# A two-layer transformer kernel on eight cores: short query tiles placed between long ones, one background piece per place, and the FFN's statistics a chunk earlier

## The reference, cut to what matters

```python
x = x + _layernorm(_L0_attn_ref(_layernorm(x), W))       # one head of width 1024
x = x + _layernorm(_L0_ffn_ref(_layernorm(x), ...))      # 1024 -> 4096 -> 1024, ternary weights
x = x + _layernorm(_L1_attn_ref(_layernorm(x), ...))     # 8 heads, causal, low-rank keys and values
x = x + _layernorm(_L1_ffn_ref(_layernorm(x), ...))      # as the layer-0 FFN, without biases

# layer 0 attention
q, k, v = jnp.split(jnp.einsum('bsd,df->bsf', x, W), 3, axis=-1)
scores = jnp.triu(jnp.einsum('bqd,bkd->bqk', q, k), k=0)
scores = jnp.where(scores == 0, MASK_NEG, scores)
out = jnp.einsum('bqk,bkd->bqd', jax.nn.softmax(scores, axis=-1), v)

# both FFNs: activations rounded to 8 bits by row, weights rounded to -1, 0, 1
scale = 127.0 / jnp.clip(jnp.max(jnp.abs(x), axis=-1, keepdims=True), EPS, None)
wq = jnp.clip(jnp.round(w / jnp.clip(jnp.mean(jnp.abs(w)), EPS, None)), -1.0, 1.0)
```

## Time and profile before

| what | value |
|---|---|
| median of 3 runs | 4179.68 us (4170.07 to 4267.94) |
| the profiled execution | 4174.65 us, its slowest core spans 4172.9 us |
| the eight cores' spans | 4144.4 to 4172.9 us |
| PE busy | 3486.8 us, 84% of the span |
| DVE busy | 2526.8 us, 61% |
| ACT busy | 1602.2 us, 38% |
| POOL busy | 900.0 us, 22% |

### The profile page before, as it was taken

How to read it: one execution, slowest core, us unless ns; L and a number is a source line. 1 busy time by engine, 2 the same in 40 slices (tenths; PEclk the granted TensorE clock), 3 DMA queues, 4 the chain that set the end, 5 groups by cost and what they waited for, 6 DMA issues and landing times.

```text
span 4172.9 us, 52221 instructions; the slowest of 8 cores (4144.4 to 4172.9 us)
## 1 busy us (share of the span) xinstructions
PE 3486.8 (84%) x16088; PEld 1544.3 (37%) x16088; DVE 2526.8 (61%) x3358; ACT 1602.2 (38%) x2230; POOL 900.0 (22%) x1111
## 2 busy tenths in 40 slices
PE   4979799872987889989826788878999699999998
PEld 1433344331333333434313333333443244444443
DVE  2423333333775667767656687877883566666674
ACT  3235554541233443334303455656778111111111
POOL 1101011123232223322224332212112111111111
PEclk9989899986998999999958899999999899999999
DMA  8558686775667788557433212122100344333332
GB/s 239 124 120 194 178 198 191 212 188 173 158 158 143 143 160 167 146 142 164 119 97 92 73 61 77 55 71 73 35 23 32 74 89 88 89 82 83 91 81 59
DMA packets 641614, 494.85 MB, mean 119 GB/s; under 512 B 536512, under 2 KB 561088, under 8 KB 640960
## 3 DMA queue, kind: packets, MB, share of 16 engines
q1 hardware_dynamic: 574752, 331.03, 34.4%
q10 hardware_dynamic: 66592, 160.49, 14.0%
HBM read 277.91 MB, written 84.93 MB: 87 GB/s over the span
## 4 chain that ended last, share of the span: by engine, by line
PE 56%; DMA 11%; DVE 10%; DVEq 6%; issue 5%; ACT 5%; POOL 3%; SPq 2%; ACTq 1%; POOLq 0%
PE psS L1358 15%; PE psO L1423 11%; PE psP L1423 10%; DVEq L1085 6%; PE psS L797 4%; PE psP L901 4%; DVE a_mx L806 3%; PE psS L410 3%; DMA a_onT<-a_on 2%; DMA hqT<-hq 2%; PE psO L881 2%; PE psO L481 2%; DMA b_stg<-w1T 2%; ACT b_stg L1118 1%; PE psP L881 1%
## 5 line engine op out<-in xcount | busy, mean ns | idle before, releaser
L806 DVE TENSOR_REDUCE a_mx<-psS 128x1 f32<-128x1024 f32 (+3 forms) x536 | 632.8, 1203 | 184.3 <-PE psS L797 142.2
L1358 PE MATMUL psS<-big,xqT 128*128 128x512 fp8e4 x2048 | 466.1, 387 | 129.9 <-DVE h L1368 76.1
L889 ACT ACTIVATE a_pT<-psO 128x512 bf16<-128x512 f32 x704 | 400.0, 598 | 225.7 <-PE psO L881 204.6
L1358 PE MATMUL psS<-a_w1q,xqT 128*128 128x512 fp8e4 x2048 | 449.0, 380 | 31.1 <-DMA xqT<-xq 28.4
L1376 ACT ACTIVATE h<-psS,st 128x1024 f32<-128x1024 f32 x128 | 142.5, 1114 | 713.9 <-PE psS L1358 641.7
L1384 DVE TENSOR_REDUCE st<-h 128x1 f32<-128x1024 f32 x256 | 304.8, 1210 | 142.5 <-ACT h L1376 142.5
L797 PE MATMUL psS<-a_kTm,a_qz 128*128 128x512 bf16 (+3 forms) x1152 | 336.1, 376 | 63.5 <-DVE a_mx L806 48.5
L410 PE MATMUL psS<-big,b_zT 128*128 128x512 bf16 (+3 forms) x1152 | 274.5, 397 | 110.9 <-ACT b_zb L391 68.6
L1358 PEld LDWEIGHTS psS<-big,xqT 128*128 128x128 bf16 x2048 | 200.1, 99 | 389.7 <-issue 167.5
L901 PE MATMUL psP<-a_pT,a_vz 128*128 128x512 bf16 x1056 | 327.0, 389 | 0.1
L1373 ACT ACTIVATE h<-h 128x1024 f32<-128x1024 f32 x128 | 135.2, 1057 | 490.3 <-DVE h L1368 487.3
(11 more groups left out here) (194 smaller groups left out, 5045.8 us busy)
## 6 DMA issues: line engine op xcount, KB each, us to landing
b_stg<-w1T ACTq DMA_DIRECT2D x64, 512.0 KB, 5.0
b_stg<-w2T ACTq DMA_DIRECT2D x64, 512.0 KB, 5.0
xt<-xres SPq DMA_DIRECT2D x64, 512.0 KB, 4.8
stg<-w1T ACTq DMA_DIRECT2D x64, 512.0 KB, 5.1
stg<-w2T ACTq DMA_DIRECT2D x64, 512.0 KB, 4.5
b_xt<-x SPq DMA_DIRECT2D x32, 512.0 KB, 5.5
b_xr<-x SPq DMA_DIRECT2D x32, 512.0 KB, 5.6
xres<-b_yz SPq DMA_DIRECT2D x32, 512.0 KB, 3.6
```

The source lines that it names most:

```text
L806: pair_free[k] = [put("v", lambda e: e.tensor_reduce(out=dst, in_=view(ps), axis=AX.X, op=ALU.max), [mm, mx_free.get(i - 2)], "v")]
L889: st_free[n] = put("s", lambda e, g=g, n=n: e.activation(out=pT[p][:, g * 512:g * 512 + 512], in_=stp[n], func=AF.Exp, bias=0.0, scale=1.0 ...
L1358: mm = put("t", lambda e, half_=half_, dc=dc: e.matmul(ps[:, half_ * 512:half_ * 512 + 512], xqT[k][:, dc, :], w1q[:, dc, c * 1024 + half_ ...
```

## The change

- The 32 tiles are visited in the order 0 to 7, then 8, 31, 9, 30, ... 15, 24, then 16 to 23 (`order`; everything is indexed by the place n, and `i = order[n]` is the tile). Where the next tile has more chunks left than the present one offers places for, its chunks are issued together ahead of the present tile's last product (`nxt`).
- `background()` runs at 144 places: after each `form_z`, after each `scores` that isn't a tile's last, after each `weigh` and after each `finish_tile`; at each it advances by 130/144 of a piece.
- `ternary` uses as many staging buffers as it gets: four in layer 0 attention, and still two in the FFN. To make room `xr` and `yz` have one buffer each.
- The four `load_w1` are issued at places 25 to 28 and wait for place 23's last scores.
- In the FFN, of both layers, `front` is split: `front_stats(t+2)` (two bn_stats, aggregate, POOL's operations) is issued at chunk 0 behind `epilogue(t-2)`; the normalising stays at chunk 1.

```diff
-                xr = [sb("xr%d" % k, [128, D], F32, ph) for k in range(2)]
-                yz = [sb("yz%d" % k, [128, D], F32, ph) for k in range(2)]
+                xr = sb("xr", [128, D], F32, ph)
+                yz = sb("yz", [128, D], F32, ph)
-                stg = [sb("stg%d" % k, [128, 1024], F32, ph) for k in range(2)]
+                stg = [sb("stg%d" % k, [128, 1024], F32, ph) for k in range(4)]
+                if NT == 32:
+                    order = list(range(8))
+                    for k in range(8):
+                        order += [8 + k, 31 - k]
+                    order += range(16, 24)
+                else:
+                    order = list(range(NT))
+                total = sum(NC - 1 - (128 * i) // CW for i in range(NT)) + 3 * NT
-                def background(cols):
-                    paid[0] += 132.0 * cols / (T * (T + 128) // 256)
+                def background():
+                    paid[0] += 130.0 / total
...
                     if c == NC - 1:
-                        zT_free[i] = mm
-                        later[0] += CW * c + CW - lo
+                        zT_free[n] = mm
                     else:
-                        background(CW * c + CW - lo)
+                        background()
...
-                for i in range(NT):
-                    if i + 2 < NT:
-                        form_z(i + 2)
-                    if i > HALF and i % 2 and len(w1_rdy) < 4:
-                        load_w1(len(w1_rdy))
+                for n in range(NT):
+                    if n + 2 < NT:
+                        form_z(n + 2)
+                    if NT == 32 and n > 24 and len(w1_rdy) < 4:
+                        load_w1(len(w1_rdy), zT_free[23])
                     mm = None
                     left = []
-                    for c in range(first(i), NC):
-                        if i + 1 < NT and c >= first(i + 1):
-                            scores(i + 1, c)
+                    nxt = list(range(first(n + 1), NC)) if n + 1 < NT else []
+                    for c in range(first(n), NC):
+                        while nxt and (nxt[0] <= c or c == NC - 1):
+                            scores(n + 1, nxt.pop(0))
                         left.append(c)
                         if len(left) > 1:
-                            mm = product(i, left.pop(0))
+                            mm = product(n, left.pop(0))
...
@@ ternary @@
+        R = len(stg)
-            lds[m] = put("s", lambda e: e.dma_start(out=stg[m % 2][:], in_=piece(wi, n)),
-                         [sfree.get(m - 2)], "bl%d" % (m % 2), 16)
+            lds[m] = put("s", lambda e: e.dma_start(out=stg[m % R][:], in_=piece(wi, n)),
+                         [sfree.get(m - R)], "bl%d" % (m % R), 16)
...
@@ ffn @@
                         if t >= 2:
                             rstd = epilogue(t - 2)
+                        if t + 2 < NT:
+                            fst_ = front_stats(t + 2)
                     if c == 1 and t + 2 < NT:
-                        rdy = front(t + 2)
+                        rdy = front(t + 2, fst_)
```

More of the change, by code:

```diff
@@ L369, in load_w1, with first, form_z @@
                         [:, :, c * 1024:c * 1024 + 1024]),
-                        [zT_free[HALF - 1]] + self.tern_rdy[0, 0], "w1c%d" % c, 16))
-                def weigh_next(i):
-                    weigh(i)
-                    background(later[0])
-                    later[0] = 0
-                def first(i):
-                    return (128 * i) // CW
-                def form_z(i):
+                        [dep] + self.tern_rdy[0, 0], "w1c%d" % c, 16))
+                def first(n):
+                    return (128 * order[n]) // CW
+                def form_z(n):
+                    i = order[n]
                     k, ps, fr = slot()
@@ L452, in weigh @@
                         row = pp[p][:, lo:CW * c + CW]
-                        n = pT_n[0] % 5
+                        m = pT_n[0] % 5
                         pT_n[0] += 1
@@ L481, in product, with finish_tile @@
                             mm = put("t", lambda e, j=j, e2=e2: e.matmul(
-                                y[:, e2 * 512:e2 * 512 + 512], pT[n][:, j, :],
+                                y[:, e2 * 512:e2 * 512 + 512], pT[m][:, j, :],
                                 vres[:, j0 + j, e2 * 512:e2 * 512 + 512],
-                                start=(c == first(i) and j == 0),
+                                start=(c == first(n) and j == 0),
                                 stop=(c == NC - 1 and j == nk - 1)),
-                                [tok, psB_free[i % 2]], "t" if last else None)
-                    pT_free[n] = mm
-                    return mm
-                def finish_tile(i, mm):
-                    k = i % 2
-                    s, b, y, zz, dd = st[i % 4], bn[k], psB[k], yz[k], dn[k]
+                                [tok, psB_free[n % 2]], "t" if last else None)
+                    pT_free[m] = mm
+                    return mm
+                def finish_tile(n, mm):
+                    i = order[n]
+                    k = n % 2
+                    s, b, y, zz, dd = st[n % 4], bn[k], psB[k], yz, dn[k]
                     ldx = put("sy", lambda e: e.dma_start(
-                        out=xr[k][:], in_=d["x"][i * 128:i * 128 + 128, :]),
-                        [x_free.get(i - 2)], "xa%d" % k, 16)
+                        out=xr[:], in_=d["x"][i * 128:i * 128 + 128, :]),
+                        [x_free.get(n - 1)], "xa%d" % k, 16)
                     for e2 in range(2):
@@ L1104, in load @@
             wi, ps, n = items[m]
-            lds[m] = put("s", lambda e: e.dma_start(out=stg[m % 2][:], in_=piece(wi, n)),
-                         [sfree.get(m - 2)], "bl%d" % (m % 2), 16)
-        load(0)
-        load(1)
+            lds[m] = put("s", lambda e: e.dma_start(out=stg[m % R][:], in_=piece(wi, n)),
+                         [sfree.get(m - R)], "bl%d" % (m % R), 16)
+        for m in range(R):
+            load(m)
         for m, (wi, ps, n) in enumerate(items):
-            k = m % 2
+            k, o = m % R, m % 2
             part = self.wpart[wi]
@@ L1287, in load_x, with front_stats @@
                     [x_free[t - NX]] if t >= NX else (), "fx%d" % (t % NX), 16)
-            def front(t):
+            def front_stats(t):
                 x, s, bn = xt[t % NX], st[t % 4], bnx[t % 2]
@@ L1481, in ffn @@
             for t in range(2):
-                quant_x(t, front(t))
+                quant_x(t, front(t, front_stats(t)))
             rdy = None
```

99 lines of the change are left out of this document (52 added, 47 removed), and 2 rows, old and new, of the table kind.

## The result

| what | before | after |
|---|---|---|
| median of 4 runs | 4177.4 us | 4275.6 us |
| lowest to highest | 4170.1 to 4267.9 | 4224.9 to 4330.5 |
| the profiled execution | 4174.65 | 4234.21 |
| mean span of its eight cores | 4157.6 | 4219.6 |

The changed kernel takes 1.0131 times as long [1.0093 to 1.0169], some 55 us more: clearly slower, but by less than 2%. The two profiled executions differ by 59.6 us.

The account below looks back on a forecast made before the run. It took ACT's pieces and casts to stall PE in the attention, and DVE's queue to set the layer 0 FFN's stall. 4174.65 - 21 + 36 + 60 = 4250, plus 5 for the median: 4255 us, range 4150 to 4315.

Parts of the forecast that it names:

- Fewer pieces among the long tiles: Layer 0 attention, first eight tiles: fewer background pieces a loop shorten stalls, and single pieces save before loop 1; -21 us.
- The pairs: Layer 0 attention, long tile beside short: little covers the long tile's transposes; 38 or 42 us a pair, +36 with last tiles.
- the price of 18.5 a loop: Last eight, two-chunk attention tiles: 3.6 rounding pieces each plus other ACT operations, 18.5 us each, 148 us in all.
- One buffer for xr and yz, four for staging: Layer 0 attention: single buffers cause no waits, upper bound +16 us; four staging buffers cost nothing beyond the first term; 0.
- Statistics a chunk ahead: Layer 0 FFN: front_stats delays the second chunk's bias, so the fourth chunk's stall grows from 2.24 to 3.75 us; +60 us.
- Three cases in four at the lower price: Layer 0 FFN: three quarters of 27 lengthened stalls have slow matmuls behind them, 1.7 us each; 34 us, so +24.
- only where hqT is late does that chain count: Layer 0 FFN: POOL's chain beside the bias makes normalising earlier, which helps only at three late-transpose waits; -4 us.
- The clock rival: Layer 0 FFN, fourth chunk: slow clock costs 2.8 us a tile, +66 in place of +24; 4297 us, chance 0.16.
- The attention near PE's work: Layer 0 attention: an even spread of pieces wins 113 of the 153 us beyond PE's work; 4127 us, chance 0.08.
- The FFN's order does nothing: Layer 0 FFN: the bias is bound elsewhere, so the split costs nothing; 4195 us, chance 0.05.
- Worse pairs: Layer 0 attention pairs: transposes land later and next scores wait for zT; 45 us a pair, +42, 4297 us, chance 0.14.

Follow-up runs that it names:

- e3: The changed kernel with the FFN statistics back at chunk 1 and the tiles in natural order 0 to 31; 1.0008 times before, attention 762.0 us on four cores.
- e5: The changed kernel with the FFN statistics back at chunk 1 and finish_tile's background piece moved behind the next cast of z; attention 748.1 us.
- e9b: As e5, but with the tiles in natural order; attention 739.2 us.
- e1: The kernel before with only the split of front (statistics at chunk 0 behind the epilogue, normalising at chunk 1); 1.0101 times before.
- e4: The kernel before with the FFN's epilogue and statistics moved behind the second chunk's bias; 4163.2 us, layer 0 FFN 1021.9 us.

## Why the prediction was right, and where it wasn't

The time was predicted at 4255 us, 1.8% more than before, within 4150 to 4315, with "within 2%" the likeliest. Measured were 4275.6 as median, 1.0131 as ratio, and for the profiled execution 4234 against the 4250 of the sum. The direction and both mechanisms are those that were forecast, the later bias and the pairs with nothing over their transposes. That the sum came within 16 us is in part luck: its terms are off by -7, +12 and -14, and the last is itself the difference of two larger errors. By its terms (the attention's from one core of each profile):

**Fewer pieces among the long tiles: -21, measured -28.** The loops of tiles 1 to 7 take 215.4 us instead of 238.2, and what lies ahead of loop 1, from the first form_z, takes 83.6 instead of 88.6. Of the stalls, 1.76, 1.95, 2.39 and 2.82 us answer to 1.5, 2.0, 2.4 and 2.8: a constant less 0.43 b, plus the length of the piece in between. Loops 5 to 7 were put at 5.0, 5.5 and 2.5 us with a rounding piece ahead of the cast each, and the first two are wrong. In loop 5 the adding-up matmul stands ahead of all this, its wait of 6.27 us took the stall's place, and 0.45 is left. In loop 6 the place was one of the empty ones, the cast starts right behind the normalising, and the stall is 1.96, which is 2.4 - 0.43. Only loop 7 has the piece, and 2.10.

**The pairs: +36, measured +48.** The eight pairs took 321.4 us, 40.2 each, where 318 was summed. A wait on pT of 4.8 to 5.8 us stands in six of them, against 4.6 in each, and stalls on the cast of 0.4 to 5.8 in all, 3.3 in the mean against 2.5. The last eight tiles took 156.8 us and not 148: the price of 18.5 a loop allowed one or two unhidden waits, and six of the eight have a cast wait of 2 to 6 us. In all the attention is 17.9 us longer, against 15 summed. e3, e5 and e9b show what stands behind it: the prediction had each mechanism, but named the wrong one as the larger. It put 4.6 us a pair, some 37 in all, on the lost cover over the transposes; undoing the order wins 9 to 14 us in all, and the piece ahead of the cast, which has 1.7 us a stall and no term of its own, costs 23 to 27.

**One buffer for xr and yz, four for staging: 0.** Not measured by itself. In e9b the attention is 18 us shorter with them.

**Statistics a chunk ahead: +60, measured +46.5.** The stall was to be 3.75 and is 3.70; it sums to +41.5 against +40. POOL's wait is 2.11 as forecast. Two sizes were off. The first is the clock: 22 to 26 of the 28 stalls of a core have slow matmuls behind them, about half of them at 5.3 us and half at 6.0 to 6.4, so +37.5 and not +24. "Three cases in four at the lower price" was too mild in both parts, in the price above all. And the six in 30 that it started from are one core's; on the eight cores it is 66 of 232, 6 to 11 a core, and 13.5 us. By the Trainium skill's rule (TensorE: Matmul & The Clock Gate, "HAM oscillation") it would have been all of them and +36. At this length of stall the trace comes near that, with 196 of 224; that the sum comes near too is chance, since fewer are slow at a higher price. At 2.24 us the trace has both levels; the page's own case has longer waits than that. The second is what the step "only where hqT is late does that chain count" made of it, -4. It looked for the gain in POOL's chain. The gain was elsewhere and larger: in the slower loop no transpose landed after more than 13.6 us, and 16.5 us of waits went, with 7 at the adding-up matmul and some 9 in `ffn2`. So the clock's 13.5 too little and the gains' 28 too little, 14 us in all, are the difference between +60 and +46.5.

**The rivals.** The clock rival asked for 2.8 us behind each of 27 stalls from a start of 10 and so for +66 in place of +24; the size was +37.5, a third of the way. The attention near PE's work is out for the change as made, but e9b shows that the even spread wins 18 us of the 153 once no piece stands ahead of the cast; the tiles that lag most were indeed those with bursts of pieces. "The FFN's order does nothing" fell with e1. "Worse pairs" fell: 40.2 and not 45 us a pair.

**Chances.** Slower by over 2% had 0.42, too much for a sum that itself lay at 1.8%; the measured ratio is below that and its interval ends at 1.7%. "Within" had 0.52 and came true.

## What to carry to other kernels

On an engine that works its queue in order, ask of each inserted operation which release stands right behind it. The same three DVE operations cost 42 us of time ahead of the bias that frees PE's slot, and moving the epilogue behind that bias too makes the stage 61 us shorter than before, together with the later folding. A background piece between two links of the chain cost its full length and the slow matmuls behind it; one operation later the attention was 27 us shorter. When a stall is taken away, look for what it was covering: here late transposes took back 49 of the 78 us that e4 had won, until one of the two streams beside them was moved. And look at a stage again with the others changed: the attention's gains were mostly lost in the FFN behind it.

## What the runs showed of the hardware

How often PE's clock falls behind a stall, and what that costs, goes with the stall's length. Behind 2.2 to 2.7 us, 16 matmuls took 5.0 to 5.3 us instead of 3.61 in 66 of 232 cases (before, eight cores). Behind 3.7 to 4.1 us they took 5.0 to 5.3 in 104 cases, 6.0 to 6.4 in 92 and 3.61 in 28 (after). So 41.5 us more of stall brought 37.5 us more of slow clock. With stalls of 0.5 us or less none of 31 was slow (e4).

A transpose of the same size, issued by the same queue, lands after 6.7 us or after up to 31.1, and which depends on what else is in flight. In e4 the rounding alone makes it at most 11.4 us, the folding beside summing pieces 15.8, folding and rounding together 18.6 in the median. In after, with a loop of 34 us, both together make it at most 13.6, and PE waits for none but the last; in a loop of 28 to 29 us it is PE's largest wait.
